# A routed mixture-of-experts kernel: 79 expert steps written out instead of looped, and the upper mask rows read back on two queues

## The chip, the cores and the metric

The kernel runs on one core of one Trainium2 chip. The metric is the device time of one execution in microseconds (us); lower is better. Names of engines: PE is TensorE (matmuls; PEld its weight loads), DVE is VectorE, ACT is ScalarE, POOL is GpSimd, SP is SyncE. A "q" behind a name is that engine's queue or sequencer.

## The reference

Two stages on x of shape (4, 1024, 256) and a context of shape (4, 77, 256). The first aligns each context with its normalised sequence by dynamic time warping: a cost matrix, a forward recursion, a backward trace of the path, and a sum of the context rows that the path gives to each position. The second is a mixture of experts with 16 experts, 2 for each token, and a shared expert.

```python
x = x + xattn(ctx_1024, layernorm(x))          # pairwise distances, DTW cost, backtrack, rows added along the path
x = x + ffn(layernorm(x), ...)

def ffn(xf):                                    # 4096 tokens, D = 256, E = 16, INTER = 128
    scores = softmax(xf @ gate_w.T)             # choice with gate_b, 2 of 4 groups, then the top 2 experts
    h = silu(xf @ We1 + be1) * (xf @ We3 + be3) # for each expert
    y = sum over the 2 experts of weight * (h @ We2 + be2)
    z = silu(xf @ ws1 + bs1) * (xf @ ws3 + bs3) @ ws2 + bs2
    return y + z
```

## The kernel before

The kernel is one program with a hand-written order for each engine; engines wait for each other on semaphores. After the alignment (up to about 180 us) the mask of the path, 128 partitions by 108 diagonals, stands skewed in SBUF. It is written to DRAM (`mask_skew`) in four cuts as VectorE finishes them, and read back straight into `maskU` in two lots of four DMAs, one for each sequence of the batch: rows 36 to 76 after the third cut has landed, and rows 0 to 35 (the upper rows) after the last. All are issued by SyncE (L448, L454). TensorE meanwhile runs 16 filler matmuls (`warm_up`, L857) and then waits for all eight reads before it transposes the mask (L949).

Then come the gate, the ranks of the tokens within their experts and the scatter of the token rows into `slot_rows` in DRAM (L593, indirect DMAs from GpSimd), so that each expert's tokens fill whole tiles of 128 rows. There are at most 79 such tiles (`SLOT_TILES`).

The expert pipeline takes the tiles one after another. For tile c:

- SyncE reads its row number from a table (L471) and loads the tile `xs` (L473), eight tiles ahead.
- TensorE transposes it (L1096), ScalarE copies the result to `xsT` (L791).
- ScalarE and VectorE copy the expert's first weights to `w_now` (L787, L1531), two tiles ahead. The expert's place is read into a register from a table, `etab` (L257).
- TensorE multiplies (L1106, eight matmul instructions), ScalarE takes the silu (L798), VectorE the product (L1543).
- TensorE multiplies with the second weights (L1116, two instructions), VectorE adds the bias and leaves `ys` (L1524), and GpSimd scatters `ys` to `results` in DRAM (L600, an indirect DMA).

On TensorE, ScalarE and VectorE the steps are given by `pipeline` (L264). It writes out the steps -2 to 14, then runs seven passes of a loop (`eng.Fori`, L267) with eight steps each, 15 to 70, and writes out the last ones. A step works on several tiles at once, for instance on the transpose of tile c + 1, the matmuls of tile c and the second matmul of tile c - 2. Inside the loop the step's number is the loop's register, so that the place in `etab`, the column of `rowf` and the values of most waits are worked out at run time; in the written-out part they are constants. SyncE's loads and GpSimd's scatters have loops of their own, of eight tiles a pass.

Of the kernel before, what the change touches and what calls it, by code (L numbers as in the profile page):

```python
# [11 lines left out]
QUAD = 32  # L12
B, S, D = 4, 1024, 256
CTX = 77
KC = D // P
CH = S // QUAD
# [3 lines left out]
NT = CTX + QUAD - 1  # L20
MASK_CUTS = (72, 36, 12, 0)
MASK_HALF = 36
# [6 lines left out]
SLOT_TILES = (2 * TOK + E * (P - 1)) // P  # L29
# [18 lines left out]
def build(nc, x, ctx, gate_w, gate_b, we1, be1, we2, be2, we3, be3, ws1, bs1, ws2, bs2, ws3, bs3, out):  # L48
# [6 lines left out]
    def sem(name):  # L55
        return nc.alloc_semaphore(name)
# [3 lines left out]
    mask_skew = nc.dram_tensor("mask_skew", (P, NT * CH), BF16, kind="Internal").ap()  # L60
# [50 lines left out]
    etab = place("etab", [P, SLOT_TILES], I32)  # L111
# [49 lines left out]
    maskU = place("maskU", [P, CTX, CH], BF16, at=cursor)  # L161
# [23 lines left out]
    rowf = place("rowf", [P, SLOT_TILES], at=cursor)  # L185
# [16 lines left out]
    xs = place("xs", [P, 8, ROW], at=cursor)  # L202
# [43 lines left out]
    b2f = b2[:, :, :].rearrange("p e d -> p (e d)")  # L246


    def live(i, c):
        return not isinstance(i, int) or 0 <= 8 * i + c < SLOT_TILES  # L250

    def head(i, c):
        return isinstance(i, int) and 8 * i + c < 0

    def load_expert(eng, regs, i, c):

        eng.reg_load(regs[c % 8], etab[0:1, bass.ds(8 * i + c, 1)])  # L257

    def expert(eng, regs, c):
        return eng.snap(regs[c % 8], min_val=0, max_val=(E - 1) * WD)  # L260

    LOOPS = (SLOT_TILES - 16) // 8

    def pipeline(eng, step):  # L264
        for c in range(-2, 15):
            step(0, c)
        with eng.Fori(1, LOOPS + 1) as i:  # L267
            for c in range(7, 15):
                step(i, c)
        for c in range(8 * LOOPS + 15, SLOT_TILES + 3):  # L270
            step(0, c)


    x_loaded = [sem(f"x_loaded{g}") for g in range(4)]
# [29 lines left out]
    mask_ready = sem("mask_ready")  # L304
    mask_out = sem("mask_out")
    mask_in = sem("mask_in")
    mask_turned = sem("mask_turned")
    maskT_ready = sem("maskT_ready")
    maskT_act = sem("maskT_act")
# [69 lines left out]
    xs_loaded = [sem(f"xs_loaded{i}") for i in range(8)]  # L379
    res_out = [sem(f"res_out{i}") for i in range(8)]  # L380
# [7 lines left out]
    results_in = results.rearrange("(p t w) d -> p t w d", t=TILES, w=2)  # L388
    out_nat = out.rearrange("b (t p) d -> p (b t) d", p=P)

    with nc.Block() as block:

        @block.sync
        def _(sp):
# [11 lines left out]
            for part, (lo, hi) in enumerate(PARTS):  # L406
                sp.wait_ge(cost_ready[part], 1)
                for b in range(B):
                    dst = bass.AP(tensor=cost_skew.tensor, offset=(b * QUAD * NT + lo) * W,
                                  ap=[[(NT + 1) * W, QUAD], [1, (hi - lo) * W]])  # L410
# [3 lines left out]
                if hi == CTX:  # L414
                    hi = NT
# [26 lines left out]
            for g in range(4):  # L442
                sp.dma_start(xk[:, 8 * g:8 * g + 8, 0:D], xn_dram[:, 8 * g:8 * g + 8, :]).then_inc(x_nat, 16)
            def read_rows(lo, hi):
                for b in range(B):
                    src = bass.AP(tensor=mask_skew.tensor, offset=(b * QUAD * NT + lo) * CH,
                                  ap=[[(NT + 1) * CH, QUAD], [1, (hi - lo) * CH]])
                    sp.dma_start(maskU[QUAD * b:QUAD * b + QUAD, lo:hi, :].rearrange("p i w -> p (i w)"),  # L448
                                 src).then_inc(mask_in, 16)

            for part, lo in enumerate(MASK_CUTS):
                hi = NT if part == 0 else MASK_CUTS[part - 1]
# [159 lines left out]
        def _(act):  # L612
# [75 lines left out]
            for T in range(TILES):  # L688
                if T >= 2:
# [13 lines left out]
            act.activation(bs2_rows[2 * QUAD:2 * QUAD + 1, :], psB[2 * QUAD:2 * QUAD + 1, :],  # L703
                           ACT.Copy).then_inc(bs2_split, 1)

            act.wait_ge(mask_turned, 4)
            for b in range(B):
                for q in (1, 3):
# [68 lines left out]

            act_expert = [act.alloc_register(f"act_expert{u}") for u in range(8)]

            def act_step_of(i, c):  # L780
                q = 8 * i + c
                if live(i, c + 2):
                    load_expert(act, act_expert, i, c + 2)
                    e = expert(act, act_expert, c + 2)
                    if not head(i, c - 2):
                        act.wait_ge(h_done, q - 1)
                    act.activation(w_now[:, (c + 2) % 4, 1, :], w13f[:, bass.ds(E * WD + e, 2 * I)],  # L787
                                   ACT.Copy).then_inc(w_act, 1)
                if live(i, c + 1):
                    act.wait_ge(x_turned, q + 2)  # L790
                    act.activation(xsT[:, (c + 1) % 2, :, :].rearrange("p c t -> p (c t)"),  # L791
                                   psX[(c + 1) % 2], ACT.Copy).then_inc(xT_copied, 1)
                if live(i, c):
                    e = expert(act, act_expert, c)
                    act.wait_ge(h_done, q + 1)
                    if not head(i, c - 2):
                        act.wait_ge(gated, q - 1)
# [30 lines left out]
        def _(pe):  # L828
# [113 lines left out]
            pe.wait_ge(nat_copied, 8)  # L942
            pe.wait_ge(mask_ready, len(MASK_CUTS))
            warm_up(16)
            pe.wait_ge(mask_in, 2 * 16 * B)
            for q in range(4):
                dst = psT[q // 2][q % 2][0:CTX, :, :].rearrange("p a b -> p (a b)").bitcast(BF16)
                for k in range(8):
# [136 lines left out]

            pe_expert = [pe.alloc_register(f"pe_expert{u}") for u in range(8)]

            def pe_step_of(i, c):
                q = 8 * i + c
                if live(i, c + 1):  # L1090
                    r = c + 1
                    pe.wait_ge(xs_loaded[r % 8], 16 * (i + r // 8 + 1))
                    if not head(i, r - 2):
                        pe.wait_ge(xT_copied, q)
# [3 lines left out]
                if live(i, c):  # L1098
                    pe.wait_ge(xT_copied, q + 1)
                    pe.wait_ge(w_act, q + 1)  # L1100
                    pe.wait_ge(w_dve, q + 1)
                    if not head(i, c - 2):
                        pe.wait_ge(gated, q - 1)
# [5 lines left out]
                if live(i, c + 1):  # L1109
                    load_expert(pe, pe_expert, i, c + 1)  # L1110
                if live(i, c - 2):
                    e = expert(pe, pe_expert, c - 2)
                    pe.wait_ge(gated, q - 1)
                    if not head(i, c - 4):
                        pe.wait_ge(y_read, q - 3)
# [17 lines left out]
        def _(dve):  # L1133
# [379 lines left out]

            dve_expert = [dve.alloc_register(f"dve_expert{u}") for u in range(8)]

            def dve_step_of(i, c):
                q = 8 * i + c
# [8 lines left out]
                if live(i, c + 2):  # L1526
                    load_expert(dve, dve_expert, i, c + 2)
                    e = expert(dve, dve_expert, c + 2)
                    if not head(i, c - 2):
                        dve.wait_ge(h_done, q - 1)  # L1530
                    dve.tensor_copy(w_now[:, (c + 2) % 4, 0, :], w13f[:, bass.ds(e, 2 * I)]).then_inc(w_dve, 1)  # L1531
                if live(i, c):
                    e = expert(dve, dve_expert, c)
                    dve.wait_ge(xs_loaded[c % 8], 16 * (i + c // 8 + 1))
                    if not head(i, c - 8):
                        dve.wait_ge(res_out[c % 8], 16 * (i + c // 8))
# [3 lines left out]
                    dve.wait_ge(silu_done, q + 1)  # L1540
                    if not head(i, c - 4):
                        dve.wait_ge(y_done, q - 3)
# [79 lines left out]
```

## Time and profile before

| what | us |
|---|---|
| median of three runs (lowest, highest) | 522.87 (520.16, 524.19) |
| the profiled execution | 518.91 |
| its span | 516.9 |
| first and last matmul of L1106 start at | 323.4 and 476.3 |
| busy: PE, DVE, ACT, POOL | 343.5, 356.7, 215.6, 154.8 |

The profile is of one execution, with times from the start of its span. The time of the execution is a little longer than the span. Busy times don't add up to the span since the engines work beside each other; in the expert pipeline TensorE, ScalarE, VectorE, SyncE and GpSimd all take part in each tile.

### The profile page before, as it was taken

Reading aid. Unit: us, or ns where it says so; the run is one execution under the profiler, and the core shown is the slowest. Engines: PE = TensorE matmul, PEld = TensorE weight load, DVE = VectorE, ACT = ScalarE, POOL = GpSimd, SP = SyncE. Lnnn points to the kernel's source line nnn. Section 1 sums busy time; section 2 is a strip of 40 time slices with the busy share of each in tenths; the row PEclk is TensorE's granted clock in tenths of the full one; section 3 lists DMA queues with packets and bytes.
Section 4 is the critical chain, followed back from the end, with each engine's and each line's share of the span. In section 5 each row is a group of like instructions: output and inputs, shape, how many; then the busy total and the mean of one; then the engine's idle time right before and its main releaser. Section 6 shows DMA issues by size and latency. Waiting matters only on the chain.

```text
span 516.9 us, 10810 instructions
## 1 busy us (share of the span) xinstructions
PE 343.5 (66%) x2360; PEld 262.5 (51%) x2361; DVE 356.7 (69%) x2007; ACT 215.6 (42%) x588; POOL 154.8 (30%) x182
## 2 busy tenths in 40 slices
PE   5851000039980977665774999977877987878974
PEld 4741000039970544333342465866766877767543
DVE  4958999999999288634483663655656665556687
ACT  2653100012229168262462312644554564554491
POOL 8000100000000003727265371244544544455200
PEclk9985555555555888889697999999999998999997
DMA  8404897950010101202122187334444533343994
GB/s 329 167 3 136 272 314 149 242 181 3 23 41 25 32 1 43 102 31 107 48 83 82 66 222 261 110 124 134 116 133 137 136 113 112 107 125 109 414 354 163
DMA packets 48362, 69.10 MB, mean 134 GB/s; under 512 B 10487, under 2 KB 38589, under 8 KB 46656
## 3 DMA queue, kind: packets, MB, share of 16 engines
q1 hardware_dynamic: 41423, 51.76, 33.2%
q0 software_dynamic: 6864, 16.86, 9.3%
q8 instruction: 15, 0.25, 0.2%
q14 instruction: 28, 0.22, 0.1%
q10 hardware_dynamic: 32, 0.02, 0.0%
HBM read 39.33 MB, written 31.24 MB: 137 GB/s over the span
## 4 chain that ended last, share of the span: by engine, by line
PE 37%; DVE 34%; issue 10%; ACT 8%; DMA 3%; another core or an unknown queue 3%; DVEq 3%; ACTq 1%; POOL 0%; SPq 0%; POOLq 0%
PE psT L1106 13%; PE psT L1004 7%; PE psT L1116 4%; DVE V L1305 3%; DVE R L1273 3%; DVE A L1311 3%; DVE M L1279 3%; PE psD L1096 2%; DVE F L1271 2%; DVE mask L1301 2%; DVE M L1269 2%; DVE A L1312 2%; PE psC L1026 2%; ACT back L809 2%
## 5 line engine op out<-in xcount | busy, mean ns | idle before, releaser
L1106 PE MATMUL psT<-xsT,w_now 128*128 128x128 f32 x632 | 86.8, 281 | 25.7 <-ACT xsT L791 25.6
L1106 PEld LDWEIGHTS psT<-xsT,w_now 128*128 128x128 f32 x632 | 77.8, 194 | 30.7 <-ACT xsT L791 23.4
L593 POOL DMA_INDIRECT slot_rows<-stage,slot x64 | 63.1, 986 | 68.3 <-DVE slot L1438 50.0
L1004 PE MATMUL psT<-x2T,sw 128*128 128x512 f32 x128 | 62.9, 637 | 0.5 <-DVE silu L1340 0.5
L600 POOL DMA_INDIRECT results<-ys_near,idx x40 | 39.4, 985 | 61.6 <-DVE ys_near L1524 51.1
L1543 DVE SCALAR_TENSOR_TENSOR hgT<-psT,w,sg 128x128 f32<-128x128 f32 x79 | 27.7, 351 | 40.5 <-ACT sg L798 27.5
L910 PE MATMUL psT<-ident,xk 128*128 128x128 f32 x64 | 15.3, 424 | 60.7 <-DMA xk<-in_x 60.7
L798 ACT ACTIVATE sg<-psT,w 128x128 f32<-128x128 f32 x79 | 28.9, 366 | 59.1 <-PE psT L1106 49.6
L1116 PE MATMUL psT<-w,hgT 128*128 x158 | 47.8, 385 | 1.2 <-DVE ys_far L1524 0.8
L600 POOL DMA_INDIRECT results<-ys_far,idx x39 | 38.4, 985 | 32.0 <-issue 16.4
L910 PEld LDWEIGHTS psT<-ident,xk 128*128 128x128 f32 x64 | 13.8, 242 | 60.7 <-issue 60.7
L683 ACT ACTIVATE xT<-psT 128x512 f32<-128x512 f32 x16 | 8.7, 594 | 84.7 <-PE psT L910 84.7
L1004 PEld LDWEIGHTS psT<-x2T,sw 128*128 128x128 f32 x128 | 25.4, 208 | 26.3 <-issue 24.5
L787 ACT ACTIVATE w_now<-w 128x256 f32 x79 | 32.9, 417 | 13.4 <-issue 11.4
L583 POOL IOTA tile_no<- 128x79 f32 x1 | 0.2, 216 | 124.1 <-PE psT L949 124.1
L1531 DVE COPY w_now<-w 128x256 f32 x79 | 24.3, 308 | 18.1 <-issue 15.4
L975 PE MATMUL psD<-ident,stage 128*128 128x128 f32 x64 | 12.5, 328 | 28.8 <-issue 23.4
L791 ACT ACTIVATE xsT<-psD 128x256 f32<-128x256 f32 x79 | 29.1, 368 | 4.8 <-PE psD L1096 4.8
L1096 PE MATMUL psD<-ident,xs 128*128 128x128 f32 x158 | 30.4, 274 | 0.3 <-issue 0.2
L720 ACT ACTIVATE x2T<-psD 128x512 f32<-128x512 f32 x16 | 9.5, 596 | 46.2 <-remote 24.0
L917 PEld LDWEIGHTS psD<-gwT,xT 128*128 128x128 f32 x128 | 28.2, 333 | 0.0
L975 PEld LDWEIGHTS psD<-ident,stage 128*128 128x128 f32 x64 | 8.8, 169 | 37.0 <-issue 28.5
(243 smaller groups left out, 816.2 us busy)
## 6 DMA issues: line engine op xcount, KB each, us to landing
xs<-slot_rows SPq DMA_DIRECT2D x79, 129.0 KB
back<-results SPq DMA_DIRECT2D x8, 1024.0 KB, 12.6
slot_rows<-fill SPq DMA_DIRECT2D x32, 129.0 KB, 5.9
xc<-in_x SPq DMA_DIRECT2D x4, 1024.0 KB, 9.2
xk<-in_x SPq DMA_DIRECT2D x4, 1024.0 KB, 12.2
out<-xk SPq DMA_DIRECT2D x7, 512.0 KB, 4.6
w<-in_L_ffn_We SPq DMA_DIRECT2D x1, 2048.0 KB, 12.9
b<-in_L_ffn_be SPq DMA_DIRECT2D x1, 2048.0 KB, 8.0
```

Source lines behind the costliest of these rows:

```text
L593: pool.indirect_dma_start(out=slot_rows, out_offset=bass.IndirectOffsetOnAxis(ap=slot[:, w, T:T + 1], axis=0), in_=stage[:, T, :], in_offs ...
L600: pool.indirect_dma_start(out=results, out_offset=bass.IndirectOffsetOnAxis(ap=idx[:, u:u + 1], axis=0), in_=ys(u), in_offset=None, bounds ...
L787: act.activation(w_now[:, (c + 2) % 4, 1, :], w13f[:, bass.ds(E * WD + e, 2 * I)], ACT.Copy).then_inc(w_act, 1)
L791: act.activation(xsT[:, (c + 1) % 2, :, :].rearrange("p c t -> p (c t)"), psX[(c + 1) % 2], ACT.Copy).then_inc(xT_copied, 1)
L798: act.activation(sg[:, c % 2, :], psH[c % 2][:, 0:P], ACT.Silu, bias=w13f[:, bass.ds(e + D, 1)]).then_inc(silu_done, 1)
L910: mm = pe.transpose(psT[n % 2][c][:, k, :], xk[:, 4 * n + k, c * P:(c + 1) * P], ident[:, :])
L917: mm = pe.matmul(psL[:, 4 * n + k, :], xT[:, n % 2, c, k, :], gwT[:, c, :], start=(c == 0), stop=(c == KC - 1))
L1004: mm = pe.matmul(psT[m][w][:, :, :].rearrange("p a b -> p (a b)"), (sw1, sw3)[w][:, c, m * P:(m + 1) * P], x2T[:, g, c, :], start=(c == 0) ...
L1096: mm = pe.transpose(psX[r % 2][:, k * P:(k + 1) * P], xs[:, r % 8, k * P:(k + 1) * P], ident[:, :])
L1106: mm = pe.matmul(psH[c % 2][:, lo:lo + P], w_now[:, c % 4, k, lo:lo + I], xsT[:, c % 2, k, :], start=(k == 0), stop=(k == KC - 1))
L1116: pe.matmul(psY[c % 2], hgT[:, (c - 2) % 4, :], w2f[:, bass.ds(e, D)], start=True, stop=True).then_inc(y_done, 1)
L1543: dve.scalar_tensor_tensor(out=hgT[:, c % 4, :], in0=psH[c % 2][:, P:2 * P], scalar=w13f[:, bass.ds(e + D + 1, 1)], in1=sg[:, c % 2, :], o ...
```

## The change

`pipeline` writes out all steps, -2 to 81, on TensorE, ScalarE and VectorE; the helpers lose the loop's register, and every place in a table and every wait is a constant. The loops of SyncE and GpSimd stay. Of the four reads of the upper mask rows, SyncE keeps the first two; ScalarE gets the other two, behind a wait for the last cut's landing, and they count on a semaphore of their own, on which TensorE waits as well.

```diff
-    LOOPS = (SLOT_TILES - 16) // 8
-
     def pipeline(eng, step):
-        for c in range(-2, 15):
-            step(0, c)
-        with eng.Fori(1, LOOPS + 1) as i:
-            for c in range(7, 15):
-                step(i, c)
-        for c in range(8 * LOOPS + 15, SLOT_TILES + 3):
-            step(0, c)
+        for c in range(-2, SLOT_TILES + 3):
+            step(c)
...
+    def mask_rows(b, lo, hi):
+        src = bass.AP(tensor=mask_skew.tensor, offset=(b * QUAD * NT + lo) * CH,
+                      ap=[[(NT + 1) * CH, QUAD], [1, (hi - lo) * CH]])
+        return maskU[QUAD * b:QUAD * b + QUAD, lo:hi, :].rearrange("p i w -> p (i w)"), src
...
             def read_rows(lo, hi):
-                for b in range(B):
...
+                for b in range(B if lo else B // 2):
+                    sp.dma_start(*mask_rows(b, lo, hi)).then_inc(mask_in, 16)
...
+            act.wait_ge(mask_out, 16 * len(MASK_CUTS))
+            for b in range(B // 2, B):
+                act.dma_start(*mask_rows(b, 0, MASK_HALF)).then_inc(mask_in_act, 16)
             act.wait_ge(mask_turned, 4)
...
-            pe.wait_ge(mask_in, 2 * 16 * B)
+            pe.wait_ge(mask_in, 16 * (B + B // 2))
+            pe.wait_ge(mask_in_act, 16 * (B - B // 2))
...
-            def dve_step_of(i, c):
-                q = 8 * i + c
-                if live(i, c - 3):
+            def dve_step_of(c):
+                if live(c - 3):
                     r = c - 3
                     e = expert(dve, dve_expert, r)
-                    dve.wait_ge(y_done, q - 2)
-                    if not head(i, r - 8):
-                        dve.wait_ge(res_out[r % 8], 16 * (i + r // 8))
+                    dve.wait_ge(y_done, c - 2)
+                    if r - 8 >= 0:
+                        dve.wait_ge(res_out[r % 8], 16 * (r // 8))
...
-                                             scalar=rowf[:, bass.ds(q, 1)], in1=xs[:, c % 8, D:D + 1],
+                                             scalar=rowf[:, c:c + 1], in1=xs[:, c % 8, D:D + 1],
```

`act_step_of` and `pe_step_of` are changed in the same way.

## Rows read from the trace of the kernel before

**Rows 1.** The page: chain by engine; instruction queues with packets, MB, share.

```profile
PE 37%; DVE 34%; issue 10%; ACT 8%; DMA 3%; another core or an unknown queue 3%; DVEq 3%; ACTq 1%; POOL 0%; SPq 0%; POOLq 0%
...
q8 instruction: 15, 0.25, 0.2%
q14 instruction: 28, 0.22, 0.1%
```

**Rows 2.** The chain in order of time, 332 to 370: start, length, what.

```profile
334.29 1.16 PE psT L1106 x8
...
336.10 0.89 PE psT L1106 x8
336.99 0.43 PE psT L1116 x2
337.43 0.22 PE psD L1096 x2
...
341.02 1.16 PE psT L1106 x8
...
347.31 1.16 PE psT L1106 x8
...
353.98 1.16 PE psT L1106 x8
...
361.56 1.16 PE psT L1106 x8
```

**Rows 3.** Timeline of ACT, 334 to 342; in brackets idle before, and releaser.

```profile
336.39 0.37 ACT L791 ACTIVATE xsT<-psD 128x256 f32<-128x256 f32 x1
339.50 0.37 ACT L798 ACTIVATE sg<-psT,w 128x128 f32<-128x128 f32 x1 [2.75 <-PE psT L1106]
```

**Rows 4.** Windows for L1106: stretch, length, busy (instructions) of PE and PEld, clock, DMA.

```profile
334.20:353.90 19.70, 9.81 (x72) 8.74 (x72) 1.00 0.40 126
353.90:463.50 109.60, 60.74 (x440) 54.44 (x440) 0.98 0.43 124
```

**Rows 5.** The chain in order of time, 366 to 415.

```profile
393.29 1.16 PE psT L1106 x8
...
399.86 1.15 PE psT L1106 x8
...
409.03 1.16 PE psT L1106 x8
```

**Rows 6.** The loop's own line, L267: count, ns min/median/max, first and last start.

```profile
L267 ACTq FUSED_REGOPS  x7: 74/74/79, 352.6 to 448.1; - x7
...
L267 PEldq COMPARE_BRANCH  x7: 76/208/243, 365.1 to 460.5; - x7
```

**Rows 7.** Timeline of DVE, written-out steps near 341 and looped ones near 384.

```profile
340.30 0.41 DVE L1524 TENSOR_TENSOR ys_far<-psT,b 128x256 f32<-128x256 f32 x1
...
341.65 0.41 DVE L1524 TENSOR_TENSOR ys_far<-psT,b 128x256 f32<-128x256 f32 x1
...
383.49 0.42 DVE L1524 TENSOR_TENSOR ys_near<-psT,b 128x256 f32<-128x256 f32 x1
...
385.34 0.42 DVE L1524 TENSOR_TENSOR ys_far<-psT,b 128x256 f32<-128x256 f32 x1 [0.37 <-issue]
...
387.03 0.42 DVE L1524 TENSOR_TENSOR ys_far<-psT,b 128x256 f32<-128x256 f32 x1
```

**Rows 8.** Timeline of POOL, the expert pipeline's scatters.

```profile
336.41 0.99 POOL L600 DMA_INDIRECT results<-ys_far,idx  x1 [0.30 <-issue]
...
386.62 0.98 POOL L600 DMA_INDIRECT results<-ys_far,idx  x1 [0.87 <-DVE ys_far L1524]
```

**Rows 9.** The chain in order of time, 168 to 182: the mask's last reads.

```profile
172.39 0.42 SPq L448
...
173.31 1.98 DMA maskU<-mask_skew
```

**Rows 10.** Timeline of PE, 169 to 176.

```profile
170.57 4.62 PE L857 MATMUL psT<-onesb 128*128 128x512 bf16 x16
175.34 0.87 PE L949 MATMUL psT<-identb,maskU 128*77 128x128 bf16 x5
```

More of the change, by code:

```diff
@@ L246, in build, with live, load_expert @@
     b2f = b2[:, :, :].rearrange("p e d -> p (e d)")
[L249 to L257, printed above, removed]
+    def live(c):
+        return 0 <= c < SLOT_TILES
+    def load_expert(eng, regs, c):
+        eng.reg_load(regs[c % 8], etab[0:1, c:c + 1])
     def expert(eng, regs, c):
         return eng.snap(regs[c % 8], min_val=0, max_val=(E - 1) * WD)
-    LOOPS = (SLOT_TILES - 16) // 8
     def pipeline(eng, step):
-        for c in range(-2, 15):
-            step(0, c)
-        with eng.Fori(1, LOOPS + 1) as i:
-            for c in range(7, 15):
-                step(i, c)
-        for c in range(8 * LOOPS + 15, SLOT_TILES + 3):
-            step(0, c)
+        for c in range(-2, SLOT_TILES + 3):
+            step(c)
     x_loaded = [sem(f"x_loaded{g}") for g in range(4)]
@@ L306, in build @@
     mask_in = sem("mask_in")
+    mask_in_act = sem("mask_in_act")
     mask_turned = sem("mask_turned")
@@ L444, in read_rows @@
             def read_rows(lo, hi):
-                for b in range(B):
[L446 to L449, printed above, removed]
+                for b in range(B if lo else B // 2):
+                    sp.dma_start(*mask_rows(b, lo, hi)).then_inc(mask_in, 16)
             for part, lo in enumerate(MASK_CUTS):
@@ L778, in _, with act_step_of @@
             act_expert = [act.alloc_register(f"act_expert{u}") for u in range(8)]
-            def act_step_of(i, c):
-                q = 8 * i + c
-                if live(i, c + 2):
-                    load_expert(act, act_expert, i, c + 2)
+            def act_step_of(c):
+                if live(c + 2):
+                    load_expert(act, act_expert, c + 2)
                     e = expert(act, act_expert, c + 2)
-                    if not head(i, c - 2):
-                        act.wait_ge(h_done, q - 1)
+                    if c - 2 >= 0:
+                        act.wait_ge(h_done, c - 1)
                     act.activation(w_now[:, (c + 2) % 4, 1, :], w13f[:, bass.ds(E * WD + e, 2 * I)],
                                    ACT.Copy).then_inc(w_act, 1)
-                if live(i, c + 1):
-                    act.wait_ge(x_turned, q + 2)
+                if live(c + 1):
+                    act.wait_ge(x_turned, c + 2)
                     act.activation(xsT[:, (c + 1) % 2, :, :].rearrange("p c t -> p (c t)"),
                                    psX[(c + 1) % 2], ACT.Copy).then_inc(xT_copied, 1)
-                if live(i, c):
+                if live(c):
                     e = expert(act, act_expert, c)
-                    act.wait_ge(h_done, q + 1)
-                    if not head(i, c - 2):
-                        act.wait_ge(gated, q - 1)
+                    act.wait_ge(h_done, c + 1)
+                    if c - 2 >= 0:
+                        act.wait_ge(gated, c - 1)
                     act.activation(sg[:, c % 2, :], psH[c % 2][:, 0:P], ACT.Silu,
@@ L1086, in _, with pe_step_of @@
             pe_expert = [pe.alloc_register(f"pe_expert{u}") for u in range(8)]
-            def pe_step_of(i, c):
-                q = 8 * i + c
-                if live(i, c + 1):
+            def pe_step_of(c):
+                if live(c + 1):
                     r = c + 1
-                    pe.wait_ge(xs_loaded[r % 8], 16 * (i + r // 8 + 1))
-                    if not head(i, r - 2):
-                        pe.wait_ge(xT_copied, q)
+                    pe.wait_ge(xs_loaded[r % 8], 16 * (r // 8 + 1))
+                    if r - 2 >= 0:
+                        pe.wait_ge(xT_copied, c)
                     for k in range(KC):
@@ L1097, in pe_step_of @@
                     mm.then_inc(x_turned, 1)
[L1098 to L1103, printed above, removed]
+                if live(c):
+                    pe.wait_ge(xT_copied, c + 1)
+                    pe.wait_ge(w_act, c + 1)
+                    pe.wait_ge(w_dve, c + 1)
+                    if c - 2 >= 0:
+                        pe.wait_ge(gated, c - 1)
                     for lo in (0, I):
@@ L1108, in pe_step_of @@
                     mm.then_inc(h_done, 1)
-                if live(i, c + 1):
-                    load_expert(pe, pe_expert, i, c + 1)
-                if live(i, c - 2):
+                if live(c + 1):
+                    load_expert(pe, pe_expert, c + 1)
+                if live(c - 2):
                     e = expert(pe, pe_expert, c - 2)
-                    pe.wait_ge(gated, q - 1)
-                    if not head(i, c - 4):
-                        pe.wait_ge(y_read, q - 3)
+                    pe.wait_ge(gated, c - 1)
+                    if c - 4 >= 0:
+                        pe.wait_ge(y_read, c - 3)
                     pe.matmul(psY[c % 2], hgT[:, (c - 2) % 4, :], w2f[:, bass.ds(e, D)],
@@ L1514, in _ @@
             dve_expert = [dve.alloc_register(f"dve_expert{u}") for u in range(8)]
-            def dve_step_of(i, c):
-                q = 8 * i + c
-                if live(i, c - 3):
+            def dve_step_of(c):
+                if live(c - 3):
                     r = c - 3
                     e = expert(dve, dve_expert, r)
-                    dve.wait_ge(y_done, q - 2)
-                    if not head(i, r - 8):
-                        dve.wait_ge(res_out[r % 8], 16 * (i + r // 8))
+                    dve.wait_ge(y_done, c - 2)
+                    if r - 8 >= 0:
+                        dve.wait_ge(res_out[r % 8], 16 * (r // 8))
@@ L1524, in dve_step_of @@
                     dve.tensor_tensor(ys(r), psY[r % 2], b2f[:, bass.ds(e, D)],
                                       ALU.add).then_inc(y_read, 1)
-                if live(i, c + 2):
-                    load_expert(dve, dve_expert, i, c + 2)
+                if live(c + 2):
+                    load_expert(dve, dve_expert, c + 2)
                     e = expert(dve, dve_expert, c + 2)
-                    if not head(i, c - 2):
-                        dve.wait_ge(h_done, q - 1)
+                    if c - 2 >= 0:
+                        dve.wait_ge(h_done, c - 1)
@@ L1531, in dve_step_of @@
                     dve.tensor_copy(w_now[:, (c + 2) % 4, 0, :], w13f[:, bass.ds(e, 2 * I)]).then_inc(w_dve, 1)
-                if live(i, c):
+                if live(c):
                     e = expert(dve, dve_expert, c)
-                    dve.wait_ge(xs_loaded[c % 8], 16 * (i + c // 8 + 1))
-                    if not head(i, c - 8):
-                        dve.wait_ge(res_out[c % 8], 16 * (i + c // 8))
+                    dve.wait_ge(xs_loaded[c % 8], 16 * (c // 8 + 1))
+                    if c - 8 >= 0:
+                        dve.wait_ge(res_out[c % 8], 16 * (c // 8))
@@ L1537, in dve_step_of @@
                     dve.scalar_tensor_tensor(out=idx[:, c % 8:c % 8 + 1], in0=xs[:, c % 8, D + 1:ROW],
-                                             scalar=rowf[:, bass.ds(q, 1)], in1=xs[:, c % 8, D:D + 1],
+                                             scalar=rowf[:, c:c + 1], in1=xs[:, c % 8, D:D + 1],
                                              op0=ALU.not_equal, op1=ALU.add).then_inc(id_copied, 1)
-                    dve.wait_ge(silu_done, q + 1)
-                    if not head(i, c - 4):
-                        dve.wait_ge(y_done, q - 3)
+                    dve.wait_ge(silu_done, c + 1)
@@ L1543, in dve_step_of @@
+                    if c - 4 >= 0:
+                        dve.wait_ge(y_done, c - 3)
                     dve.scalar_tensor_tensor(out=hgT[:, c % 4, :], in0=psH[c % 2][:, P:2 * P],
```

## The prediction

> **What bounds the kernel now.** I read the page first, for the chain's shares: no engine carries it alone, and a tenth of it is time in which an engine waits for nothing that the profile shows [rows 1]. So the expert pipeline has to be read by itself. I took the chain in order of time there. On TensorE a step is three pieces: eight matmuls of L1106 (0.89 us), two of L1116 (0.43) and two transposes of L1096 (0.22), in sum 1.54 us [rows 2]. If TensorE alone set the pace, 79 steps would take 122 us. They don't keep that pace: the pieces that last 1.16 us instead of 0.89 are those that begin after a stall, and they start at 334.29, 341.02, 347.31 and 353.98 [rows 2]. Between two such starts lie three steps, so a group of three costs (353.98 - 334.29) / 3 = 6.56 us, of which 4.6 are TensorE's and about 1.9 a stall.
>
> Where the stall begins is seen on ScalarE. The silu of L798 sits idle for 2.75 us before 339.50, and its releaser is the matmul [rows 3], which by the chain was done some 2 us before; TensorE then stands still because the copy of xsT comes late. I don't know what holds up the signal. It returns every few steps, while GpSimd sends one indirect scatter after another.
>
> Now the point that decides: the pipeline already has both forms of code in it. Steps 0 to 14 of the three engines are written out in the kernel before, steps 15 to 70 are seven passes of a loop, steps 71 to 78 are written out again, while SyncE's loads and GpSimd's scatters run in loops throughout. That is, the stretch 334.2 to 353.9 is already what the change makes of the whole. The windows give 72 matmuls of L1106, 9 steps, in 19.70 us there: 2.19 us a step. The stretch 353.9 to 463.5, mostly looped, has 440, 55 steps, in 109.60 us: 1.99 a step [rows 4]. The written-out stretch is the slower one.
>
> The chain further on tells why. In a pass of the loop, restarts stand at 393.29, 399.86 and 409.03 [rows 5]: a group of three in 6.57 us, the same as in written-out code, and a group of five in 9.17, 1.83 a step. The group of five is the one that begins with the branches.
>
> **The change part by part.**
> *Branches and register work, removed.* A branch costs TensorE 0.21 us, seven times [rows 6]. If all of it were on the path: 7 x 0.21 = 1.5 us saved; if it hides under the stall, after which it comes, 0. I take 0, since the groups of three cost the same with and without it.
>
> *Step addresses and wait values that are constants.* VectorE gets faster while it catches up after a stall: in written-out code two adds of L1524 start 1.35 us apart (340.30 and 341.65); in the loop, across the branch, 1.85 (383.49 and 385.34), and the next 1.69 [rows 7]. TensorE sets the long-run pace, so these 0.3 to 0.5 us buy nothing by themselves. But they set how densely GpSimd issues: it is idle 0.30 us before a scatter in the written-out stretch and 0.87 after the branch [rows 8]. My reading is that the stall comes back when the scatters stand back to back, so that the slow start after a branch is what stretches a group from three steps to five. With the cover gone, the stall comes sooner.
>
> *The sum for 55 steps.* All groups of three: 18.33 x 6.56 = 120.3 us against 109.6, +10.7. A group of four exists too, 353.98 to 361.56, 7.58 us [rows 2]; all fours: 13.75 x 7.58 = 104.2, -5.4. I take 15 threes and two and a half fours (SyncE's and GpSimd's branches stay and may stretch a group now and then): 98.4 + 19.0 = 117.4, +7.8. It lies near the threes because the written-out stretch shows nothing else. Leaving and entering the loop I take as nothing, between -0.2 and +0.2 us (one branch).
>
> *More code to stream.* The two instruction queues moved 0.25 MB in 15 packets and 0.22 MB in 28 over the span [rows 1]. The seven passes stand in the code once now; if a pass fills one or two packets, some ten more are needed (an estimate). The written-out stretch already runs code for the first time, and what that costs is in its 6.56. Bounds beyond it: 0 if the loading hides, and one stall, 1.9 us, for each of ten if none does, +19; I take 0, since in the written-out stretch nothing lies between the restarts but TensorE's own 1.54 a step. The Trainium skill speaks for this change here: "Runtime: NRT & Kernel Launch", section Instruction fetch mechanics, says that code is fetched in sequence and that a taken branch out of the window held makes the engine wait for a fetch, so that full unrolling is preferred. By it the loop would pay at its branches; the trace shows the stalls in written-out code as often or oftener.
>
> *Mask rows.* The last four reads of the skewed mask are issued by SyncE one after another, the second at 172.39 and the last at 173.31, and land 1.98 us after the last [rows 9]. With two each on SyncE and ScalarE, the last is issued at about 172.4, or 172.5 if ScalarE needs 0.42 for each as SyncE does: 0.8 to 0.9 us earlier. What is late next is TensorE itself: its 16 filler matmuls of L857 start at 170.57 and last 4.62, to 175.19, and the first transpose of L949 starts at 175.34 [rows 10]. So 0.15 us is saved, 0.3 if the last filler's modelled end is too late; 0.9 if the cover were gone. Below nothing: ScalarE's queue would have to hold the reads up. Its new wait on mask_out stands ahead of its share of the mask copies, which wait for the transposes anyway; +0.5 us is the bound (one more issue). I take -0.2.
>
> Sum: +7.8 - 0.2 = +7.6. The profiled execution took 518.91 us (span 516.9), so 526.5; the runs' median is 522.87, 4 us above it, and with the same difference I give **530.5 us**. A measurement of this kernel can hardly tell less than 1% (5.2 us) from nothing; its three runs lie 4 us apart.
>
> **The rivals.**
> *The five stays (25%).* What stretches the group could be the branches of SyncE's and GpSimd's loops, which stay, and which fall into the same groups. Against it: in 334 to 354 these loops turned as well, and no group grew. Then the pipeline keeps 1.99 a step and the time is 522.7, within 3 us.
>
> *Fewer stalls (17%).* If each stall is due after so much work of the sequencers, address arithmetic among it, then constants let a group run longer. All fours give -5.4 - 0.2: 517.3; all groups like the five, 55 x 1.83 = 100.9, -8.7 - 0.2: 514.0. Against it: the written-out groups have that work removed already and are the shortest.
>
> *The stalls are the loop's own (7%).* Then two in each of seven passes go: a pass takes 15.74 [rows 5] and would take 8 x 1.54 = 12.3, which gives -24 and 498.7. This is the outcome by the skill's rule above. Against it stand the restarts at 341 and 347, before ScalarE has entered its loop at 352.6 [rows 6].
>
> *Code streaming is exposed (6%).* Ten blocks at a stall each: +19, 542. It decides as soon as a block arrives later than its engine needs it, which the stretch from 334 to 354 doesn't show.
>
> **How the numbers follow.** The forecast has 45%: threes throughout would give 533.4, some fours 528, so its own range is 526 to 534. Faster by over 1% needs a result under 517.6: most of the fewer-stalls case and the loop's own, 22% in all. Within 1% (517.6 to 528.1): the case in which the five stays, and the lower end of the forecast and the upper of fewer stalls, 31%. Slower: 47%. The range leaves out the loop's own, and the worst of code streaming: 514 to 537.
>
> **What the profile would show.** If I am right, the chain of the changed kernel has restarts of 1.16 us every third step from 334 on to about 470, 6.5 to 6.7 us apart; the windows count 8 matmuls each 2.1 to 2.2 us; GpSimd's idle time before a scatter is 0.3 to 0.4 except behind a stall; and the last matmul of L1106, which starts at 476.3 now by the table of times, starts near 484. The mask is right if the last read lands by 174.6 and the transposes still start at 175.0 or later. I am wrong if restarts lie four or more steps apart: then the head's short groups came from the start-up and not from the form of the code. A step of over 1.6 us without a restart would point to code loading.

## The result, and the profile after

The changed kernel takes **530.23 us**, the median of six runs (527.55 to 534.95); the kernel before, on the same chip, 523.20 (520.16 to 524.37). The ratio is 1.0185 [1.0146, 1.0223]; here and below the ratio is estimated from the fast runs with a 95% interval, and isn't the quotient of the medians, which is 1.013 here. So the change made the kernel slower, by 1.3% at the medians and 1.9% by the ratio. The forecast was 530.5. The profiled execution took 527.55 us with a span of 525.6, so 8.7 us of span are to be found. In the changed file the lines of the pipeline are L1101 (L1106 before), L1111 (L1116), L1091 (L1096), L793 (the silu, L798), L786 (the copy of xsT, L791), L1518 (the adds, L1524) and L593 (the scatters, L600).

Where they went is read from the first and last matmul of L1101, in the view of that line:

```profile
L1101 PE MATMUL psT<-xsT,w_now x632: 274/275/581, 322.4 to 485.2; 128*128 128x128 f32 x158
```

It spans 162.8 us; L1106 spanned 152.9 before (323.4 to 476.3 in the table). So the pipeline costs 9.9 us more, it begins 1.0 us earlier, and what lies behind it is 0.2 us shorter: 9.9 - 1.0 - 0.2 = 8.7.

The chain in order of time, to lay beside [rows 2] and [rows 5]; start, length, what:

```profile
335.90 1.16 PE psT L1101 x8
...
342.17 1.16 PE psT L1101 x8
...
387.39 1.16 PE psT L1101 x8
...
393.81 1.16 PE psT L1101 x8
...
432.83 1.16 PE psT L1101 x8
...
457.64 1.16 PE psT L1101 x8
```

A step that begins with 1.16 us is a restart after a stall. From 335.90 to 432.83 there are sixteen of them, always three steps apart: 96.93 / 15 = 6.46 us a group. No group of five is left in this stretch. In the whole pipeline, counting as a restart each step that starts over 2 us after the one before, there were 20 before and there are 24 now. Behind 432.83 the chain is less regular: the next twelve steps, to 457.64, take 24.81 us, 2.07 each. Both kernels have an odd place in common, three restarts at steps 57 to 59 with a chain that runs through an unknown queue; it costs about the same in both and is no part of the difference.

The windows for L1101, as in [rows 4] (stretch, length, busy and instructions of PE and PEld, clock, DMA share, GB/s):

```profile
334.20:353.90 19.70, 9.84 (x73) 8.74 (x72) 1.00 0.41 127
353.90:463.50 109.60, 56.43 (x408) 50.30 (x408) 0.98 0.39 116
353.90:470.00 116.10, 59.70 (x432) 53.21 (x432) 0.99 0.39 117
```

In the head the window counts nine steps, as before. The long stretch counts 408 matmuls, 51 steps, in the time in which 55 passed before: 2.15 us a step for 1.99. The third line reaches to 470 and is used below.

ScalarE's wait is where it was [rows 3], still with TensorE's matmul as its releaser:

```profile
360.23 0.37 ACT L793 ACTIVATE sg<-psT,w 128x128 f32<-128x128 f32 x1 [2.76 <-PE psT L1101]
```

And GpSimd's scatters, as in [rows 8]. Idle time 0.30 means that the next was issued as soon as it could be, 1.29 us after the one before; only behind a stall (2.90) is there more:

```profile
357.13 0.98 POOL L593 DMA_INDIRECT results<-ys_far,idx  x1 [0.30 <-issue]
...
362.31 0.98 POOL L593 DMA_INDIRECT results<-ys_near,idx  x1 [2.90 <-DVE ys_near L1518]
```

The page's instruction queues [rows 1] took 21 and 35 packets for 15 and 28. So more packets of code are loaded, but between 335 and 432 a step that isn't followed by a restart takes 1.55 or 1.65 us, as before:

```profile
q8 instruction: 21, 0.34, 0.3%
q14 instruction: 35, 0.29, 0.2%
```

**The mask rows** did come on two queues. Timelines of SyncE, ScalarE and TensorE, 169 to 176:

```profile
169.49 0.34 SPq L447 DMA_DIRECT2D mask_skew<-mask  x1
171.13 0.78 SPq L442 DMA_DIRECT2D maskU<-mask_skew  x2
...
171.95 0.38 ACT L696 ACTIVATE bs_rows<-psC 1x256 bf16<-1x256 f32 x1 [1.74 <-PE psC L934]
171.96 0.79 ACTq L701 DMA_DIRECT2D maskU<-mask_skew  x2
...
171.71 4.38 PE L852 MATMUL psT<-onesb 128*128 128x512 bf16 x16
175.93 0.35 PE L945 MATMUL psT<-identb,maskU 128*77 128x128 bf16 x2
```

ScalarE is in the middle of its work on the bias rows and sends its two reads 0.83 us behind SyncE's. TensorE's fillers, which now begin at 171.71, end at 176.09 as they are modelled, and the first transpose starts at 175.93. ScalarE's second read is issued at about 172.4 (171.96 and half of 0.79) and, landing 1.98 later as in [rows 9], is there at 174.3 (an estimate), 1.8 us before the fillers end. In the kernel before the last read landed at 175.29 (173.31 + 1.98 [rows 9]), 0.1 us behind the fillers' end at 175.19 [rows 10]. So the reads did come out of the way, by the 0.1 us that they had stood in it.

### The profile page after: what moved, and what is told of

It is laid out like the page before. It is cut to its first block, busy times and chain, and to the rows that moved or that the text cites. A ratio compares the mean times of both kernels' runs of the same rounds, so it can differ in the third digit from the quotient of the medians.

```text
span 525.6 us, 10469 instructions
## 1 busy us (share of the span) xinstructions
PE 341.5 (65%) x2360; PEld 260.4 (50%) x2360; DVE 351.6 (67%) x2006; ACT 213.5 (41%) x587; POOL 154.8 (29%) x182
## 4 chain that ended last, share of the span: by engine, by line
PE 45%; ACT 15%; SPq 9%; DVE 9%; another core or an unknown queue 8%; issue 7%; DMA 5%; ACTq 2%; POOLq 0%; DVEq 0%; POOL 0%
PE psT L1101 17%; PE psD L912 5%; PE psT L1000 5%; PE psT L1111 4%; PE psT L905 3%; ACT psC L684 2%; SPq L416 2%; DMA xk<-in_x 2%; PE psD L1091 2%; ACT stage L721 2%; PE psC L1022 2%; SPq L421 2%; ACT back L804 2%; SPq L439 2%
## 5 line engine op out<-in xcount | busy, mean ns | idle before, releaser
L1101 PE MATMUL psT<-xsT,w_now 128*128 128x128 f32 x632 | 87.0, 281 | 34.8 <-ACT xsT L786 31.7
L1101 PEld LDWEIGHTS psT<-xsT,w_now 128*128 128x128 f32 x632 | 77.5, 193 | 41.2 <-ACT xsT L786 38.1
L793 ACT ACTIVATE sg<-psT,w 128x128 f32<-128x128 f32 x79 | 28.9, 366 | 74.3 <-PE psT L1101 66.0
L593 POOL DMA_INDIRECT results<-ys_near,idx x40 | 39.4, 986 | 61.9 <-DVE ys_near L1518 45.7
L593 POOL DMA_INDIRECT results<-ys_far,idx x39 | 38.4, 985 | 41.0 <-DVE ys_far L1518 31.1
L1111 PE MATMUL psT<-w,hgT 128*128 x158 | 47.5, 384 | 0.7 <-DVE ys_far L1518 0.7
L786 ACT ACTIVATE xsT<-psD 128x256 f32<-128x256 f32 x79 | 29.3, 371 | 6.6 <-remote 2.9
L1525 DVE COPY w_now<-w 128x256 f32 x79 | 23.8, 301 | 11.0 <-issue 3.1
L1091 PE MATMUL psD<-ident,xs 128*128 128x128 f32 x158 | 30.4, 274 | 0.2 <-issue 0.2
L1335 DVE SCALAR_TENSOR_TENSOR silu<-psT,sb,silu 128x512 f32<-128x512 f32 x16 | 12.0, 748 | 23.4 <-ACT silu L732 18.4
```

Of the source, the lines that this page charges most:

```text
L593: pool.indirect_dma_start(out=results, out_offset=bass.IndirectOffsetOnAxis(ap=idx[:, u:u + 1], axis=0), in_=ys(u), in_offset=None, bounds ...
```

## The experiments

All on kernels that differ from the one before or the changed one by the edit shown. Each ratio is against the kernel before, run beside it on the same chip. Runs 1 to 4 were on one chip, 5 to 8 on a second, 9 to 11 on a third and 12 on a fourth.

**1. Unrolling alone.** The kernel before, the three engines written out, the mask left as it was.

```diff
+    def pipeline(eng, step, out=False):
+        if out:
+            for c in range(-2, SLOT_TILES + 3):
+                step(0, c)
+            return
-            pipeline(act, act_step_of)
+            pipeline(act, act_step_of, out=True)   # and pe, dve
```

> The kernel before with the expert steps written out on three engines and the mask reads left as they were. Theory (the form of the step code shortens the groups from five steps to three): everything of the +7 to +10 us is here, groups of three all through, 6.4 to 6.6 us each, ratio to before 1.014 to 1.022. Rival (the second queue for the mask, or its place in ScalarE's order, costs something): under 1.01.

Measured: 529.41 us, 1.0164 [1.0101, 1.0226]. Its window (416 matmuls, 52 steps, where the kernel before has 55) for the matmul, and its restarts in the chain, again three steps apart:

```profile
353.90:463.50 109.60, 57.63 (x416) 51.52 (x416) 0.98 0.39 117
```

```profile
387.39 1.16 PE psT L1110 x8
...
393.90 1.16 PE psT L1110 x8
```

The unrolling alone gives the loss, within the interval of the whole change.

**2. The mask alone.**

```diff
-                for b in range(B):
+                for b in range(B if lo else B // 2):
+            act.wait_ge(mask_out, 16 * len(MASK_CUTS))
+            for b in range(B // 2, B):
+                act.dma_start(*mask_rows(b, 0, MASK_HALF)).then_inc(mask_in_act, 16)
```

> The kernel before with the mask reads on two queues and the looped pipeline. Theory: the filler matmuls and what stands ahead of them cover it, -0.3 to +0.3 us, ratio 0.998 to 1.002; the last read lands 0.8 to 0.9 us after the landing of the cut sooner than before. Rival (a real gain hidden in the sum of the change): 0.9 us, ratio 0.998 or less; not told apart by the times alone, but by the first transpose's distance from the last cut.

Measured: 523.76 us, 1.0030 [0.9998, 1.0063]. In its timelines both queues send at the same moment, and still nothing comes of it. ScalarE's two issues, and the chain with fillers and transposes:

```profile
170.86 0.84 ACTq L711 DMA_DIRECT2D maskU<-mask_skew  x2
```

```profile
169.34 5.81 PE psT L863 x16
...
175.14 2.96 PE psT L956 x23
```

From the last cut's issue to the first transpose it is 175.14 - 169.22 = 5.92 us here and 175.93 - 169.49 = 6.44 in the changed kernel. The same distance is 175.34 - 170.38 = 4.96 in the kernel before, but 176.15 - 170.32 = 5.83 in run 4, whose four reads are all on SyncE. So it doesn't go by the queues; it seems to go by the fillers, which last 4.62 us in the kernel before, 5.71 in run 4 and 5.81 here, or, in the changed kernel, start 2.2 us behind the cut. There is no gain, at most a loss of some tenths of a per cent.

**3 and 4. Which engine's branch is it?** In 3 only VectorE is written out; in 4 TensorE and ScalarE are, and VectorE stays looped.

```diff
-            pipeline(dve, dve_step_of)              # 3
+            pipeline(dve, dve_step_of, out=True)
-            pipeline(pe, pe_step_of)                # 4, and act
+            pipeline(pe, pe_step_of, out=True)
```

> The kernel before with the steps written out on VectorE alone; TensorE and ScalarE keep their loops. Theory as I wrote it (VectorE's slow start behind its branch spaces the scatters and stretches the group): groups of three throughout, idle time of GpSimd before a scatter 0.3 us, as slow as all three written out, ratio 1.013 to 1.022. Rival 1 (the branches of TensorE or ScalarE do it): fives stay, ratio 0.997 to 1.003.

> The kernel before with the steps written out on TensorE and ScalarE; VectorE keeps its loop. Theory (VectorE's branch stretches the group): groups of three and five in turn as before, ratio 0.997 to 1.003. Rival 1 (TensorE's or ScalarE's branches): threes throughout, 1.013 to 1.022. If e3 and e4 both lie half way, it takes the branches of more than one engine.

Measured: 3 gives 529.71 us, 1.0132 [1.0065, 1.0198]; 4 gives 519.88, 0.9964 [0.9933, 0.9994]. The windows for the matmul, first of 3 (404 of them), then of 4 (440, as before):

```profile
353.90:463.50 109.60, 55.00 (x404) 48.98 (x405) 1.00 0.38 114
```

```profile
353.90:463.50 109.60, 61.42 (x440) 55.29 (x440) 0.97 0.44 125
```

GpSimd's scatters behind a stall, in 3:

```profile
382.30 0.98 POOL L604 DMA_INDIRECT results<-ys_near,idx  x1 [2.96 <-DVE ys_near L1528]
383.59 0.99 POOL L604 DMA_INDIRECT results<-ys_near,idx  x1 [0.30 <-issue]
...
388.79 0.98 POOL L604 DMA_INDIRECT results<-ys_far,idx  x1 [2.90 <-DVE ys_far L1528]
```

and in 4, where VectorE has its branch between the first and the second:

```profile
383.62 0.98 POOL L604 DMA_INDIRECT results<-ys_near,idx  x1 [2.75 <-DVE ys_near L1528]
385.48 0.98 POOL L604 DMA_INDIRECT results<-ys_far,idx  x1 [0.88 <-DVE ys_far L1528]
387.16 0.98 POOL L604 DMA_INDIRECT results<-ys_far,idx  x1 [0.70 <-issue]
388.61 0.98 POOL L604 DMA_INDIRECT results<-ys_far,idx  x1 [0.46 <-issue]
```

In 3 the scatters start 1.29 us apart, the third 1.31 behind the second, and the next stall comes after three. In 4 they start 1.86, 1.68 and 1.45 apart, and the group has five steps. From step 17 on run 3 has no group longer than three but one of four, though TensorE, ScalarE, SyncE and GpSimd all turn in loops. So VectorE's loop makes the group of five; the loops of the others make none. The edit takes VectorE's register work away together with its branch, and no run parts the two: of the distances in 4, 1.86 spans the branch, 1.68 and 1.45 don't. 4 is also the one version whose time lies under that of the kernel before, by 0.4%.

**5 and 6. Without the scatters.** In 5 GpSimd only counts, and `results` is filled with zeros ahead: the experts' part is missing from the output. In 6 the loads of the tiles after the first eight are left out as well.

```diff
-                pool.indirect_dma_start(out=results, ...).then_inc(res_out[u], 16)
+                pool.sem_inc(res_out[u], 16)
```

> The changed kernel without the expert pipeline's scatters of results (GpSimd only counts res_out up; the results in DRAM are filled from a constant tile earlier, so the output lacks the experts' part). Theory (GpSimd's indirect scatters hold up signals of the other engines): no restarts in the pipeline, 1.55 us a step, first to last matmul about 122 to 126 us instead of 163. Rival (SyncE's loads, or the code itself): the stalls stay, every third step.

> As e5, and SyncE loads only the first eight tiles, so that the pipeline works on stale tiles and moves no data at all. Theory: same as e5, 1.55 us a step. Rival (loads cause stalls): this one is free of stalls and e5 is not. If both have stalls, the cause lies in the instructions of the compute engines.

Measured: 489.00 and 485.71 us, one run each. The matmul in 5:

```profile
L1101 PE MATMUL psT<-xsT,w_now x632: 270/275/422, 326.1 to 448.2; 128*128 128x128 f32 x158
```

122.1 us for 79 steps, 1.55 each: TensorE's own pace. With the loads and without the scatters nothing stalls from the fourth step on. Leaving out the loads as well takes off 3.3 us more, from one run each.

**7 and 8. A small gap.** One memset of 128x128 on GpSimd ahead of each scatter, in the changed kernel (7) and in the one before (8).

```diff
+                pool.wait_ge(gap_step, 8 * i + u + 1)
                 pool.sem_inc(passed, 1)
+                pool.memset(gap[:, :], 0.0).then_inc(gap_step, 1)
```

> The changed kernel with a memset of 128x128 on GpSimd ahead of every scatter of results (0.2 us and its own issue, so that scatters stand 1.5 to 1.6 us apart instead of 1.29). Theory (a stall comes back when scatters stand back to back): the groups get longer or the stalls go, and the kernel gets faster, by 10 to 30 us. Rival (a stall is due after so many scatters or so much work, however dense): groups of three remain, the time within 1% of the changed kernel's, or longer because GpSimd becomes the bound at 1.6 us a tile.

> The same memset in the kernel before (looped). Theory: its groups of three and five get longer or the stalls go; as e7 or better. Rival: within 1% of the kernel before.

Measured: 533.36 us, 1.0230 [1.0149, 1.0311], and 522.03, 1.0016 [0.9983, 1.0049]. The gap came out smaller than I aimed at, since most of the memset went into the 0.30 us that were idle anyway. GpSimd in 7:

```profile
351.64 0.98 POOL L597 DMA_INDIRECT results<-ys_near,idx  x1 [0.16 <-issue]
...
353.01 0.98 POOL L597 DMA_INDIRECT results<-ys_near,idx  x1 [0.17 <-issue]
```

At 1.37 us apart the groups of three stay. So 7 says that 0.08 us more is not enough. In 8, where the looped groups of five are spaced more widely anyway, nothing changed.

**9. A wide gap.** Two memsets of 128x256 in bf16 ahead of each scatter of the changed kernel.

```diff
+                for part in range(2):
+                    pool.wait_ge(gap_step, 16 * i + 2 * u + 1 + part)
+                    pool.sem_inc(passed, 1)
+                    pool.memset(gap[:, :], 0.0).then_inc(gap_step, 1)
```

> The changed kernel with two memsets of 128x256 bf16 on GpSimd ahead of every scatter of results, so that scatters stand about 1.8 us apart where they follow each other at once (the single memset of e7 spaced them by no more than 1.37). Theory (stalls come back when scatters stand close): groups of five or more or no stalls, 79 x 1.8 = 142 us for the pipeline against 162, the kernel 10 to 20 us under the changed one and under the kernel before. Rival (the load of the step, not the distance of the scatters, brings the stall): threes stay, and the time is that of the changed kernel or above.

Measured: 541.55 us, 1.0409 [1.0335, 1.0483]. The scatters came out 2.19 to 2.21 us apart, more than aimed at (timeline of GpSimd, with the second of the two memsets):

```profile
331.78 1.00 POOL L598 DMA_INDIRECT results<-ys_near,idx  x1 [0.44 <-POOL gap L597]
...
333.26 0.31 POOL L597 MEMSET gap<- 128x256 bf16 x1 [0.15 <-POOL gap L597]
333.99 0.98 POOL L598 DMA_INDIRECT results<-ys_near,idx  x1 [0.42 <-POOL gap L597]
```

and the windows for the matmul:

```profile
330.00:350.00 20.00, 13.73 (x104) 12.63 (x104) 1.00 0.48 137
353.90:463.50 109.60, 55.26 (x392) 47.44 (x392) 1.00 0.39 114
```

In 330 to 350, while the ring of buffers still holds room, TensorE makes 104 / 8 = 13 steps in 20 us, 1.54 each, with no stall, though a scatter goes out all the while. Once the ring is full, 2.19 us a tile on GpSimd is the bound, hence 49 steps in the long stretch and the loss. The time is a miss: 10 to 20 us less than the changed kernel were expected. What the run shows is in its first seventeen steps; in the changed kernel the stalls begin with the eighth.

**10 and 11. Bytes, or the loads?** 10 scatters 16 of 256 columns to a table of its own, with `results` filled ahead (experts' part missing); 11 loads only the two index columns of every tile from the ninth on, so that those tiles are computed from stale rows.

```diff
-                    in_=ys(u), ...                                    # 10
+                    in_=ys(u)[:, 0:16], ...
-                sp.dma_start(xs[:, u, :], slot_rows[bass.ds(at, P), :])        # 11
+                sp.dma_start(xs[:, u, D:ROW], slot_rows[bass.ds(at, P), D:ROW])
```

> The changed kernel whose scatters of results move 16 of the 256 columns, to a table of their own (as many indices and rows, a sixteenth of the bytes; the output lacks the experts' part). Theory a (what GpSimd does for each index holds up the others): threes at 6.4 to 6.5 us as in the changed kernel. Theory b (the bytes of the scatter on the DMA engines do it): no stalls, pipeline 120 to 126 us.

> The changed kernel whose loads of tiles 8 and up bring only the two index columns of each row (tiles' data stay those of the first eight, so the output's expert part is not the reference's); scatters are whole. Theory (scatters alone suffice): stalls stay, groups of three or near it, pipeline 150 to 163 us. Rival (loads and scatters together do it): few or no stalls, 120 to 130 us.

Measured: 525.74 and 531.33 us, one run each. Windows for the matmul, of 10 and of 11 (last column GB/s, 116 in the changed kernel):

```profile
353.90:463.50 109.60, 56.58 (x408) 50.56 (x408) 0.98 0.26 68
```

```profile
353.90:463.50 109.60, 56.20 (x407) 50.21 (x406) 0.98 0.20 57
```

Half the traffic, and the same 51 steps. Neither the bytes of the scatters nor those of the loads make the stall. In 11 the loads are still issued, and no run has scatters without any loads.

**12. The gap in between, on another chip.** One add of 128x224 on GpSimd ahead of each scatter of the changed kernel.

```diff
+                pool.tensor_tensor(gap[:, :], fill[:, 0:224], fill[:, 0:224], ALU.add).then_inc(gap_step, 1)
```

> The changed kernel with one add of 128x224 on GpSimd ahead of every scatter of results, for a distance of about 1.75 us between scatters, which lies between 1.37 (e7: threes as ever) and 2.19 (e9: no stall in the first steps, but GpSimd is the bound). Theory (a scatter leaves something behind that takes about 1.8 us to drain, and the stall comes when two or three have piled up): the stalls go or come every eight steps or more, the pipeline takes 138 to 148 us instead of 162 and the kernel 505 to 516 us, under both. Rival (only distances over 2 us are free of stalls): threes to fives remain, 525 us or more.

Measured: 470.36 us against **454.50** for the kernel before on this chip (452.26 to 456.93, eleven runs), 1.0348 [1.0303, 1.0393]. The kernel before is 67 us faster here than on the three chips of runs 1 to 11. The expected numbers were for such chips, so the run doesn't test what it was meant to. On this chip I find no stall at all, in the pipeline, where the scatters are 1.76 us apart, or ahead of it. There the token scatters go out 1.27 us apart, and the windows of all engines, 205 to 225 (busy and instructions of PE, PEld, DVE, ACT, POOL), read in this kernel

```profile
205.00:225.00 20.00, 17.72 (x84) 10.64 (x82) 15.26 (x55) 16.60 (x39) 15.14 (x16) 0.91 0.29 106
```

and in the kernel before on the first chip

```profile
205.00:225.00 20.00, 12.24 (x44) 6.63 (x43) 8.79 (x34) 6.51 (x14) 11.86 (x13) 0.84 0.24 87
```

The first and the last of the 64 token scatters start at 200 and 281 us here, and at 200 and 311 in the kernel before on the first chip. So back-to-back scatters are not enough for a stall: the chip has a part in it. In the pipeline the tiles pass every 1.76 us, GpSimd's spacing, and it takes 132.7 us from first to last matmul. If the kernel before keeps TensorE's own pace on this chip (122.1, run 5), that is 10.6 of the 15.9 us lost; the rest I haven't traced. Neither the changed kernel nor, with a trace, the one before was run on this chip, so what the change is worth there is open.

## Why the prediction was right

**Direction and size.** Said: groups of three nearly throughout, +7.8 us for the stretch of 55 steps, 530.5 in all. The windows give 54 steps in 116.10 us (353.90 to 470.00: 432 matmuls), so 55 take 118.2 against the 117.4 of the sum and 109.6 before. The threes were shorter than I took them, 6.46 for 6.56. Of the two and a half groups of four one came, at 432.83, and it runs into the odd place at steps 57 to 59, which the sum left out; with it and the six free steps behind it, twelve steps took 2.07 us each where threes take 2.15. These errors nearly cancel. That the medians agree within 0.3 us (530.5 and 530.23) is luck besides: the six runs spread over 7.4 us, the medians differ by 7.0 and the two profiled executions by 8.6, for a forecast of 7.6. The other 1.3 us of the pipeline's 9.9 lie outside the stretch: a restart more at step 78 of the tail was in no term. The sign that I named, restarts every third step to about 470, held to 432.83, and again from 457.64 to 470.58.

**The reason.** Said: VectorE's slow start after a branch spaces the scatters and so stretches a group. Runs 3 and 4 show that VectorE's loop alone does it, its branch and its register work together, with the spacing beside it, and run 1 that nothing else of the change is needed. That the spacing is the link, and not something else in VectorE's loop, rests on run 5 (no scatters, no stall) and run 9 (2.19 apart, none in seventeen steps), with VectorE written out in both. Run 9 is the one that changes the spacing, by more work on GpSimd, and it speaks for the start of the pipeline alone; no run packs the looped kernel's scatters closer with VectorE's loop in place. So the link is well supported, but in part argued. Two places in the trace of the changed kernel, where VectorE is written out too, bear on it. Timeline of GpSimd:

```profile
331.26 0.98 POOL L593 DMA_INDIRECT results<-ys_near,idx  x1 [0.52 <-issue]
332.81 0.98 POOL L593 DMA_INDIRECT results<-ys_near,idx  x1 [0.56 <-issue]
336.40 0.98 POOL L593 DMA_INDIRECT results<-ys_far,idx  x1 [2.61 <-DVE ys_far L1518]
...
448.46 0.99 POOL L593 DMA_INDIRECT results<-ys_near,idx  x1 [1.17 <-issue]
450.10 0.98 POOL L593 DMA_INDIRECT results<-ys_near,idx  x1 [0.65 <-issue]
452.02 0.98 POOL L593 DMA_INDIRECT results<-ys_near,idx  x1 [0.93 <-issue]
```

The pipeline's first four scatters (328.20 to 332.81) go out at TensorE's own pace, 1.51 to 1.55 us apart, and a stall follows; in the kernel before one follows after the first three (329.25, 330.79, 332.31). So the prediction's "back to back" is too narrow: at 1.55 us apart a stall still comes. From 446.83 to 454.56, where the scatters stand up to 2.15 apart, six steps pass without one. With the groups of five, 1.40 to 1.86 apart, this fits a backlog that grows when scatters come faster than one in about 1.8 to 2.2 us (an estimate from these distances and run 9); no run shows what the backlog would be.

**Branches at nothing.** TensorE's branches were costed at 0, as hidden. Run 4 took them out with ScalarE's, with VectorE's kept: -0.4%, 2.1 us at the median, and its interval takes in the 1.5 us that seven branches cost. So 0 was perhaps somewhat low. In the changed kernel it can't be told apart.

**Code loading at nothing.** Thirteen packets more, about the ten estimated, and no step over 1.65 us between a restart and the stall before the next. By the Trainium skill's "Runtime: NRT & Kernel Launch", Instruction fetch mechanics, written-out code was to be preferred; here full unrolling lost 1.6% (run 1), and writing out TensorE and ScalarE alone gained 0.4% (run 4).

**The mask.** Said: -0.2 us. No gain shows, with the transposes later than 175.0 and the last read before 174.6 as foretold. Run 2 alone gives +0.3%, its interval just touching 1. In the changed kernel ScalarE's share is issued 0.83 us late, which the sum had only as a bound.

**The rivals.** The five stays: gone by the chain, and by run 3, in which GpSimd's and SyncE's loops turned as ever. Fewer stalls: there are four more. The stalls are the loop's own: same. Code streaming: above.

**Not foreseen.** The pipeline began 1.0 us earlier in the profiled execution; I haven't traced it to a cause.

**Open.** What holds up TensorE's signal to ScalarE during the scatters. It is neither the scatters' bytes (run 10) nor the loads' (run 11), and it needs the scatters (run 5), by all that is shown at a short distance (run 9), and a chip that has it (run 12). Whether other work beside the scatters has a part, VectorE's copies of `w_now` (L1525) above all, no run tests: every version keeps them on VectorE.

## What to carry to other kernels

When a change turns a loop into straight code, look whether the old trace already has a straight stretch beside the looped one, and compare the time of a step: here the answer was 2.19 against 1.99 us. Making an engine that is not the bound faster can cost time, by packing what it feeds (here GpSimd's indirect scatters) more densely; ask for each instruction removed what its delay was holding apart. And compare kernels on the same chip only: one chip ran the kernel before in 454.5 us, the others took 522 to 523.

## What the runs showed of the hardware

- Not every chip has the stall. The kernel before took 521.6 to 522.0 us on the three chips of runs 1 to 11 and 454.5 on the fourth, where the trace of run 12 has no stall.
- An indirect scatter keeps GpSimd 0.98 us whether it moves 16 columns or 256. Timeline of GpSimd in run 10:

```profile
340.36 0.98 POOL L597 DMA_INDIRECT thin<-ys_far,idx  x1 [0.36 <-issue]
```

- With an add on GpSimd ahead of each scatter, VectorE's copies from SBUF to SBUF take 646 ns in the mean, against 301. The two runs are on different chips; that it is the add and not the chip rests on VectorE's adds from PSUM, which take 409 ns there against 424. Group of L1525 in the changed kernel; its counterpart in run 12, and one of the adds (busy us, mean ns, idle before):

```profile
L1525 DVE COPY w_now<-w 128x256 f32 x79 | 23.8, 301 | 11.0 <-issue 3.1 <-PE psT L1101 0.4
```

```profile
L1530 DVE COPY w_now<-w 128x256 f32 x79 | 51.1, 646 | 2.0 <-issue 0.7
...
L1523 DVE TENSOR_TENSOR ys_near<-psT,b 128x256 f32<-128x256 f32 x40 | 16.4, 409 | 0.0
```

The Trainium skill's "GPSIMD Engine Reference", Specifications, says that GpSimd shares its SBUF interface with VectorE and contends with some of its modes. The rows agree that the two engines hold each other up.
